# Attention block of an eight-stage kernel: keys and values computed by channel, biases in the evictions, part of the 3x3 convolution on ScalarE and GpSimd

## What is computed

```python
qkv = _conv(x, qkv_w, qkv_b)                                   # 1x1, 64 -> 192
s3 = _conv(_conv(qkv, dw3_w, dw3_b, groups=C3, pad=1), pw3_w, pw3_b, groups=HEADS)
s5 = _conv(_conv(qkv, dw5_w, dw5_b, groups=C3, pad=2), pw5_w, pw5_b, groups=HEADS)
att = _relu_linear_att(concatenate([qkv, s3, s5], axis=1))     # three scales
x = x + _conv(att, proj_w, proj_b)
# _relu_linear_att, per head of 8 channels: q, k = relu(q), relu(k); v gets a row of ones
# vk = v k^T over the pixels; out = vk q; out[:8] / (out[8] + 1e-15)
```

## Time and profile before

| | us |
|---|---|
| runs | 632.06, 626.96, 631.44 (median 631.44) |
| profiled execution, its own time | 627.8 |
| its span, first to last instruction | 626.0 |
| first stage in it (SP issues the load of the next block at) | 134.24 |
| mean granted clock of TensorE over the span | 0.947 of full speed |

### The profile page before, as it was taken

One profiled execution on the slowest core, in us unless ns is written; L12 is line 12 of the kernel. 1 busy time (PEld: TensorE's weight loads), 2 busy tenths in 40 slices (PEclk: granted clock), 3 DMA queues, 4 the chain that ended last, 5 costly groups with the idle time before them and its releaser, 6 DMA issues. The chain is left out here.

```text
span 626.0 us, 12008 instructions
## 1 busy us (share of the span) xinstructions
PE 517.0 (83%) x5122; PEld 283.1 (45%) x5122; DVE 359.7 (57%) x574; ACT 284.4 (45%) x392; POOL 147.2 (24%) x140
## 2 busy tenths in 40 slices
PE   3889989977997975777888888757997898699994
PEld 1463347834224875776777542313333234333231
DVE  2344894255665458978867357474337696722534
ACT  2452222236551229999899336543671102333230
POOL 9900000010002002887977500015003002000000
PEclk9999999998999997999998887876999999799998
DMA  7000000020001006654552000110003000000000
GB/s 273 1 3 2 3 0 2 1 98 1 0 1 31 2 9 230 193 189 151 186 177 101 1 19 0 49 39 0 0 2 109 1 0 0 2 0 1 0 18 17
DMA packets 7989, 29.90 MB, mean 48 GB/s; under 512 B 864, under 2 KB 2176, under 8 KB 7552
## 3 DMA queue, kind: packets, MB, share of 16 engines
q1 hardware_dynamic: 7936, 29.14, 13.8%
HBM read 28.47 MB, written 0.67 MB: 47 GB/s over the span
## 5 line engine op out<-in xcount | busy, mean ns | idle before, releaser
L1009 PE MATMUL PS<-GX,OH 128*128 128x64 f16 x2304 | 76.1, 197 | 26.8 <-DVE OH L1171 17.7
L1009 PEld LDWEIGHTS PS<-GX,OH 128*128 128x128 f16 x2304 | 73.2, 101 | 31.7 <-issue 18.9
L1096 ACT ACTIVATE DIST<-BC,wbuf 128x2048 f16<-128x2048 f16 x24 | 48.0, 2001 | 2.2 <-DMA BC<-idx_dram 0.5
L1898 DVE TENSOR_SCALAR HID<-PS,wbuf 128x512 f32<-128x512 f32 x32 | 23.8, 750 | 41.6 <-PE PS L1791 41.6
L1171 DVE TENSOR_SCALAR OH<-BC,wbuf 128x2048 f16<-128x2048 f16 x48 | 45.2, 965 | 2.6 <-DMA BC<-idx_dram 2.6
L1099 ACT ACTIVATE OH<-DIST 128x2048 f16<-128x2048 f16 x24 | 45.9, 1911 | 0.9 <-PE PS L1009 0.2
L944 POOL TENSOR_TENSOR V<-SQ 128x512 f32<-128x512 f32 x18 | 28.2, 1569 | 58.8 <-DVE SQ L1182 58.1
L144 PE MATMUL PS<-X,wconst 128*128 128x512 f32 x32 | 20.3, 768 | 23.4 <-DMA wconst<-pack_dram 9.1
L1837 ACT ACTIVATE HID<-PS,wbuf 128x512 f32<-128x512 f32 x32 | 22.0, 687 | 36.2 <-PE PS L1791 36.2
L163 ACT ACTIVATE SQ<-PS 128x512 f32<-128x512 f32 x16 | 9.6, 597 | 63.5 <-PE PS L144 63.5
L1787 PE MATMUL PS<-Y,wbuf 64*128 64x512 f32 x128 | 36.5, 615 | 2.2 <-DVE HID L1898 1.5
(11 more groups left out here) (301 smaller groups left out, 954.6 us busy)
## 6 DMA issues: line engine op xcount, KB each, us to landing
BC<-idx_dram SPq DMA_DIRECT2D x36, 512.0 KB, 4.5
wbuf<-pack_dram SPq DMA_DIRECT2D x1, 2082.5 KB, 11.1
wbuf<-pack_dram SPq DMA_DIRECT2D x1, 1656.0 KB, 7.3
wbuf<-pack_dram SPq DMA_DIRECT2D x1, 1494.5 KB, 6.3
wbuf<-pack_dram SPq DMA_DIRECT2D x1, 820.0 KB, 12.6
wconst<-pack_dram SPq DMA_DIRECT2D x1, 759.5 KB, 6.7
wbuf<-pack_dram SPq DMA_DIRECT2D x1, 732.0 KB, 4.0
wbuf<-pack_dram SPq DMA_DIRECT2D x1, 602.5 KB, 3.8
```

The lines of the kernel that those rows point to most:

```text
L1009: mm = pe.matmul(o, OH[:, s % NOH, qh, t * P:(t + 1) * P], src, start=(qh == 0 and part == 0), stop=(qh == 1 and part == 1))
L1096: after_act(act, act.activation(DIST[:, :], BC[:, s % NBC, :], ACT.Abs, bias=wt("negq1")))
L1898: dve.tensor_scalar(HID[:, n % 8, :], bank(2 + n % 4), wt("b1_3", 2 * e + m, 1), 0.0, ALU.add, ALU.max).then_inc(hid_in_v, 1)
```

## The change

In the first stage:

- The bias matmuls L358 and L378 go, with `BPARTS`, `INSIDE`, `ONEB` and POOL's work for them, and 579 of the columns of `wconst`. The bias of T is now added in the evictions: ACT with `Identity` and a bias, DVE with `tensor_scalar` in place of a copy. This makes T wrong outside the image, so POOL multiplies its rim by a mask of 0 and 1 (four `tensor_scalar` of 272 elements for each j), and each `conv(t)` waits for that.
- Keys and values are computed by channel, `keys_values(s, i)`: the weights are the stationary operand and each matmul has 512 columns. ACT and DVE evict with bias and ReLU into `KVC`, in instructions over 64 partitions. PE then turns them, `by_pixels(s, u)`: eight 128x128 transposes, which ACT evicts in one copy for each bank. `Y` and its copies go.
- Of the three 3x3 blocks two go from `BLOCKS`. Their taps, with the one on DVE, are five (`EDGE3`). ACT writes the first of them, scaled and with the bias, into `D3[j]`, and the first edge tap of the 5x5 likewise into `D5[j]` (`begin(j)`); it writes the other four into two buffers `TAP` (`taps`), from which POOL adds them to `D3[j]`, twelve `tensor_tensor` of 1024 elements in all. The results of `conv(t)` are no longer evicted by ACT; DVE adds each bank to `D5[j]` or `D3[j]` (`folded(t)`), for a 3x3 after POOL's four adds.
- Tasks 2 and 3 change places, `conv(0)` runs before the transposes of scale 0, and the numerators of scale 0 go to other banks (`MBANK`).

Everywhere: nine semaphores for the weights become three (one for pack 0, one for the odd packs, one for the even ones), with thresholds from `W_AT`.

```diff
-BLOCKS = [(5, 0, 0), (5, 0, 2), (5, 2, 0), (5, 2, 2), (3, 1, 1), (3, 1, 3), (3, 3, 1)]
+BLOCKS = [(5, 0, 0), (5, 0, 2), (5, 2, 0), (5, 2, 2), (3, 1, 1)]
+EDGE3 = [(dy, dx) for dy in range(3) for dx in range(3) if dy == 2 or dx == 2]
-            TASKS = [(0, 5), (0, 3), (1, 3), (1, 5), (2, 3), (2, 5)]
+            TASKS = [(0, 5), (0, 3), (1, 5), (1, 3), (2, 3), (2, 5)]
 gpsimd
+                for n in range(3 * (NE3 - 1)):
+                    j = n // (NE3 - 1)
+                    pool.wait_ge(begun, 2 * j + 2)
+                    pool.wait_ge(tap_in, n + 1)
+                    pool.tensor_tensor(D3[j][:, :], D3[j][:, :], TAP[n % NTAP][:, :], ALU.add).then_inc(tap_used, 1)
+                    pool.wait_ge(tap_used, n + 1)
 tensor
+                def keys_values(s, i):
+                    if s == 0:
+                        pe.wait_ge(t_act, 18)
+                        pe.wait_ge(t_dve, 18)
+                    elif s == 2:
+                        pe.wait_ge(att_ready, 2)
+                    taps = 1 if s == 0 else 3
...
+                            mm = pe.matmul(bank(2 * i + g), w, src, start=(j == 0), stop=(j == taps - 1), tile_position=(a, 0))
+                def by_pixels(s, u):
+                    pe.wait_ge(kvc_act, KVC_ACT[s])
+                    pe.wait_ge(kvc_dve, KVC_DVE[s])
...
+                                mm = pe.transpose(bank(2 * u + g)[:, (2 * h + i) * P:(2 * h + i + 1) * P], KVC[s][g][:, at:at + P], wt("ident"))
                 pe.wait_ge(conv_in, 12)
-                pe.wait_ge(d3_ready, 3)
 scalar
+                def taps(j, first, last):
+                    for i in range(first, last):
+                        n = j * (NE3 - 1) + i - 1
+                        dy, dx = EDGE3[i]
+                        if n >= NTAP:
+                            act.wait_ge(tap_used, n - NTAP + 1)
+                        act.activation(rows(TAP[n % NTAP][:, :]), window(QKVP[j], 1 + dy, 1 + dx), ACT.Identity,
+                                       scale=wt("dw3e", j * NE3 + i, 1)).then_inc(tap_in, 1)
 vector
-                    dve.tensor_copy(o, src).then_inc(t_dve, 1)
+                    dve.tensor_scalar(o, src, wt("bqt", u // 3, 1), None, ALU.add).then_inc(t_dve, 1)
+                def folded(t):
+                    j, k = TASKS[t]
+                    d = (D3 if k == 3 else D5)[j]
+                    dve.wait_ge(begun, 2 * j + 2)
+                    if k == 3:
+                        dve.wait_ge(tap_used, (NE3 - 1) * (j + 1))
+                    for n in range(2):
+                        c = slice(n * HC, (n + 1) * HC)
+                        dve.wait_ge(conv_ps, 2 * t + n + 1)
+                        dve.tensor_tensor(d[:, c], bank(DBANK[t % 3] + n), d[:, c], ALU.add).then_inc(conv_in, 1)
```

More of the change, by code:

```diff
@@ L99, in build @@
         x_in = sem("x_in")
-        w_in = [sem(f"w_in{n}") for n in range(len(SECTIONS))]
+        w_sems = [sem(f"w_in{n}") for n in range(3)]
+        w_in = [w_sems[0 if n == 0 else 2 - n % 2] for n in range(len(SECTIONS))]
+        W_AT = [16 if n == 0 else 16 * ((n + 1) // 2) for n in range(len(SECTIONS))]
         stored = sem("stored")
@@ L219, in build @@
             RD = sb("RD", [P, PIX], F32, sctx)
[L220 to L225, removed]
+            NTAP = 2
+            TAP = [sb(f"TAP{i}", [P, COLS], F32, sctx) for i in range(NTAP)]
             TR = H + 3
@@ L284, in _ @@
                     pool.memset(QKVP[j][:, :, :], 0.0).then_inc(prepared, 1)
-                pool.memset(ONEB[:, :], 1.0)
                 pool.memset(VK[:, :, :, :], 0.0).then_inc(prepared, 1)
[L287 to L306, removed]
+                pool.memset(ones_of(0), 1.0).then_inc(prepared, 1)
+                pool.wait_ge(w_in[1], W_AT[1])
                 for j in range(3):
@@ new lines, in keys_values @@
+                    for j in range(taps):
+                        for g in range(2):
+                            a = C * g
+                            if s == 0:
+                                src, w = window(YP[a:a + C], 2 + 8 * i, 2, 8), wt("wkv", 0, P, a, a + C)
+                            else:
+                                src, w = (D3, D5)[s - 1][j][a:a + C, i * HC:(i + 1) * HC], wt("pwkv", ((s - 1) * 3 + j) * P, P, a, a + C)
+                            mm = pe.matmul(bank(2 * i + g), w, src, start=(j == 0), stop=(j == taps - 1), tile_position=(a, 0))
@@ L469, in queries @@
                     mm.then_inc(q_ps, 1)
+                for i in range(2):
+                    keys_values(0, i)
                 pe.wait_ge(prepared, DIAG_SET)
+                conv(0)
                 for u in range(2):
-                    kv_unit(0, u)
-                conv(0)
+                    by_pixels(0, u)
+                conv(1)
                 vk(0)
-                conv(1)
+                conv(2)
                 den(0)
-                for t in range(2, 6):
+                for t in range(3, 6):
                     conv(t)
                 pe.wait_ge(conv_in, 12)
-                pe.wait_ge(d3_ready, 3)
                 queries(1)
-                kv_unit(1, 0)
-                kv_unit(1, 1)
+                for i in range(2):
+                    keys_values(1, i)
                 numerators(0)
+                for u in range(2):
+                    by_pixels(1, u)
                 inverse(0)
@@ L490, in _ @@
                 queries(2)
-                kv_unit(2, 0)
+                for i in range(2):
+                    keys_values(2, i)
                 den(1)
-                kv_unit(2, 1)
                 numerators(1)
+                for u in range(2):
+                    by_pixels(2, u)
                 inverse(1)
@@ L1963, in pack_weights @@
     for i in range(2):
-        diag2("wkv", qkv_w[ch[1 + i]].T, i * P)
+        twice("wkv", qkv_w[ch[1 + i]].T, i * C)
+    quarter = np.arange(P) // 32
+    put("rim", np.stack([quarter // 2 == 1, quarter // 2 == 0, quarter % 2 == 1, quarter % 2 == 0], 1).astype(f))
+    for j in range(3):
+        for hf in range(2):
+            put("bqt", np.tile(v["L0_conv_qkv_b"][ch[j]][32 * hf:32 * hf + 32], 4)[:, None], 0, 2 * j + hf)
     for s, (w, b) in enumerate((("qkv_w", "qkv_b"), ("pw3_w", "pw3_b"), ("pw5_w", "pw5_b"))):
@@ L1986, in pack_weights @@
         put("headspread", heads.T, 32 * bl, bl * P)
-    rows("brows", np.concatenate([v["L0_conv_qkv_b"][c] for c in ch] + [v["L0_conv_" + b][ch[o]] for b in ("qkv_b", "pw3_b", "pw5_b") for o in (1, 2)]))
-    put("pmask", np.tile(np.eye(C, 3, dtype=f), (2, 1)))
     put("id32", np.tile(np.eye(32, dtype=f), (4, 1)))
```

258 lines of the change are left out of this document (134 added, 124 removed).

## The result

| | before | after |
|---|---|---|
| median of 17 runs, us | 628.28 (623.66 to 632.06) | 636.47 (630.78 to 641.19) |
| ratio to before, 95% interval | | 1.0125 (1.0095 to 1.0155) |
| profiled execution, its span | 626.0 | 637.4 (its own time 639.23) |
| granted clock over the span | 0.947 | 0.927 |

What follows compares the result with a forecast made beforehand. DVE was taken as the bound, with PE full beside it: +11.4 to X, -1.0 behind it and +1.8 for the slow clock make +12.2 on 627.8, so 640.0, named as 641 us; range 621 to 650.

Steps and rivals of the forecast that it cites:

- The term that decides: POOL's ten additions beside DVE's sixteen edge taps before X exclude each other: 8.3 additions cost DVE 19.0 us.
- Rival 1: No exclusion between POOL's additions and DVE's edge taps: X at 81.4, total 622.4 us; chance 0.25.
- rival 2: No exclusion, but POOL additions of 3.1 us: X at 88.6, total 629.6 us, no change; chance 0.10.
- X: Point in the first stage where PE starts queries(1): 87.62 us before, forecast at 99.0, +11.4.
- Rival 3: T unit evictions bind at today's pace, losing 2.0 us of gain: 643.1 with exclusion, 625.5 without; chance 0.05.
- The signs: Trace marks of being right: overlapped edge taps or additions of 3.5 us, PE idle from about 79 to 99 us.
- Start: PE's first matmul waits for the wconst load, now smaller: 1.1 us sooner, bounds 0 and 2.6.
- the rims: POOL's masking of T's rim, four tensor_scalar for each j, 0.6 us each, ending before DVE's edge taps.
- From the first edge tap to X: DVE's piece from 48.8 us: sixteen edge taps, 19.0 us of exclusion, mask, ten L669 and a reciprocal, ending at 99.0.
- Behind X: From queries(1) to the end of the third vk: 36.0 instead of 37.0 us, before 1.8 us for the slow clock.
- the cold clock: After PE's idle time before X, queries(1) runs at the lower clock level: 1.8 us added.
- The chances: Odds for the whole program: slower 0.56 (above 637.8 us), faster 0.20 (below 625.1), same 0.24.

Runs made afterwards that it cites:

- experiment 1: Changed kernel with both 3x3 blocks back on TensorE, only the corner tap on ACT, no POOL additions; 616.89 us, ratio 0.9868.
- experiment 2: Changed kernel with POOL's additions replaced by a memset of the same 1024 elements, writing only; 616.15 us, ratio 0.9845.
- 4: Changed kernel with POOL's additions cut from 1024 to 16 elements, waits and signals kept; 616.06 us, ratio 0.9861.
- 7: Changed kernel with one of the two 3x3 blocks back on TensorE, so six POOL additions instead of twelve; 627.39 us, ratio 1.0004.
- experiment 8: Changed kernel with DVE's 24 edge taps as tensor_scalar products with one SBUF input, POOL's additions kept; 624.63 us, ratio 0.9959.
- experiment 3: Changed kernel with POOL's additions replaced by a tensor_scalar copy that reads one tile of 1024 elements; 628.4 us, ratio 1.0015.
- 6: Changed kernel with the twelve added 3x3 taps computed on DVE, none on ACT and POOL; 634.57 us, ratio 1.0119.
- 9: Changed kernel with both 3x3 blocks back on TensorE, plus the first 5x5 edge tap back on DVE; 617.38 us, ratio 0.984.
- 10: Changed kernel with both 3x3 blocks back on TensorE, plus ACT's begin(0) moved behind keys_values(0); 614.81 us, ratio 0.9805.
- 5: Kernel before the change with only the weight loads' semaphores reduced to three; 626.83 us, ratio 0.9995.

## Why the prediction was right

- **The term that decides** held. I took the whole length of each addition, 8.3 x 2.28 = 19.0 us; measured 9.3 x 1.94 = 18.06. That the products are so near is in part luck: there were more additions beside edge taps than I laid out by hand (5.3 in the first eight taps, not 3), and each cost less than its length. Experiments 1, 2, 4 and 7 show that it is POOL's reading that costs, in proportion to the additions. The prediction had both kinds of DVE operation that lose, the fast one from L1171 and the one with two SBUF inputs; it was my theory for experiment 8 that left the first out. The Trainium skill, "SBUF — State Buffer", section "Who interferes with whom", has both: there a GpSimd instruction that only writes does not contend (experiment 2 agrees, 1285 ns), and `tensor_scalar` in a two-port mode does (experiment 8 agrees). That the second one blocks fully fits the additions nearly (1.94 to 2.1 of 2.4 us), not the copies of experiment 3 (0.66 of 2.8).
- **Rivals.** 1 and 2 said no exclusion, and the edge taps of 2038 ns in the mean refute both. Rival 1 priced X at 81.4, where POOL's chain ended, and the time at 622.4 us. No experiment is its case: in 2 and 4 X comes at 81.36 and 78.20 and the time is 616, but POOL's operations are shorter there. The 3.1 us that rival 2 gave an addition were there (3.06 in the mean), as a consequence of the exclusion. Rival 3 fell: 18 T units took 13.06 us, 12.9 forecast.
- **The signs.** An addition beside edge taps took 3.2 to 3.3 us (3.5 said) and an edge tap up to 3.34. PE was idle before X from 86.4 us on, not from 79: I had it ready by 73, but it had stood still for 10.7 us up to 74.04, since the mask that `den(0)` waits for stands on DVE behind the first eight edge taps. That cost X nothing, as DVE was later still.
- **Start: the term with the wrong sign.** The load was sooner by 0.64, not 1.1 us, but the T units began at 28.58 instead of 25.7:

```profile
8.42 3.75 PE L148 MATMUL PS<-X,wconst 128*128 128x512 f32 x4 [8.42 <-DMA wconst<-pack_dram]
...
14.74 3.04 PE L158 MATMUL PS<-SD,wconst 128*128 128x128 f32 x16 [1.46 <-DVE SD L182]
19.09 7.04 PE L325 MATMUL PS<-YP,wbuf 128*128 128x512 f32 x12 [1.31 <-DVE YP L187]
...
28.58 8.00 PE L348 MATMUL PS<-YP,wbuf 64*32 64x408 f32 x192 [1.38 <-ACT QR L533]
```

In experiment 1, with the same code up to here:

```profile
14.61 2.05 PE L158 MATMUL PS<-SD,wconst 128*128 128x128 f32 x16 [1.46 <-DVE SD L182]
18.07 5.39 PE L325 MATMUL PS<-YP,wbuf 128*128 128x512 f32 x12 [1.41 <-DVE YP L187]
...
25.91 8.00 PE L348 MATMUL PS<-YP,wbuf 64*32 64x408 f32 x192 [1.39 <-ACT QR L533]
```

The same matmuls take 2.6 us more in the changed kernel's profile, where from 10 to 20 us the granted clock is 0.78; it is 1.00 in that of experiment 1 and 0.73 in that of experiment 2. From PE's first matmul to its first T unit it is 17.6 us in experiments 1, 4, 7 and 8, and 18.6 to 20.2 in the changed kernel and in 2, 3, 6, 9 and 10, all with the same code up to there. So no edit of an experiment makes it. The two profiles with the old start (before and 5) have 17.7; whether the change makes the long start more frequent stays open. So does its cause in part: in 6 and 10 L158 takes 3.44 and 3.61 us at a granted clock of 1.00. The first edge tap so came at 52.25, not 48.8; of these 3.4 us, 2.9 are this start, and the pieces behind it hit within 0.3 us each, though the rims took 0.97 us each where I said 0.6. Of the +12.5 us to X in this profile 2.5 are the long start (20.2 against 17.6), not the stage behind it.
- **From the first edge tap to X**: 50.2 forecast, 47.9 measured. 0.9 is the exclusion, 1.0 the L669 that follow each other at 0.62, not 0.72 us. So X = 99.0 against 100.12 is luck in part: two errors that offset each other.
- **Behind X** I was 3.6 us too high: 37.8 with the cold clock, 34.17 measured.

```profile
L380 PE MATMUL PS<-wconst,KVC 128*128 128x128 f32 x32 | 3.9, 274 | 1.1 <-ACT KVC L568 1.1
```

These are the 32 transposes of two scales, each recorded as one pass. I had read the 32 of L971 as 16 transposes of two passes each, like the f32 matmuls, and priced the 16 of a scale at 3.9 us where they take 1.97: 3.9 us too much in two scales. The cold `queries(1)` was right, 4.90 against 2.93 us in the earlier trace rows, 1.8 forecast.
- **The chances**: slower by over 1% had 0.56, and the ratio is 1.0125. The sum on the profiled execution, 640.0, met 639.23, and that nearness is luck too: behind X and from the first edge tap to X I was 5.9 us too high, up to the first edge tap (3.4) and in the seven stages behind (+1.7, put at nothing) 5.1 too low. By the medians the change costs 8.2 us, not 12.2. The medians of the two kernels lie 3 to 4.5 us below what the forecast was set against (631.44 then, 628.28 over 17 runs) and what it named (641).

## What to carry to other kernels

POOL is not a free engine beside a DVE that reads two SBUF tiles or runs a fast `tensor_scalar`: an addition of two f32 tiles took 1.94 to 2.1 us from it, almost its own length of 2.43, so work moved there from TensorE landed on the engine that was already full. Give POOL what only writes, or let it run beside DVE work that reads PSUM, and look at the minimum and the mean of the neighbour's instruction, not at POOL's share. Ask too what the engine that gives work away does with the time: here PE only waited, its clock fell, and most of what X had won (3.1 us) was lost again behind X (2.3 to 2.5). In a change of many parts, undo the one that feeds the full engine first: here that turned +1.25% into -1.3%.

## What was not expected

- A POOL `tensor_scalar` copy of 1024 f32 took 2.8 us by itself (two in 5.63), an addition of two such tiles 2.43. The simpler operation is the slower one, yet it takes 0.66 us from DVE where the addition takes 1.94. Why it holds DVE up so much less stays open.
- A fast DVE `tensor_scalar` of 1024 f32 (755 ns alone) lost as much to an addition as a two-input operation of 1285 ns: a single one took up to 2.81 us.
- Transposes of 128x128 f32 are one pass in the records, 0.12 us apart, against two for a matmul.
